# An attention and expert block on one core: a PSUM bank for the softmax denominators, three banks for the row scores, and a new order of the matmuls and copies

## The reference

```python
x = x + _layernorm(_L0_attn_ref(_layernorm(x), w_qkv, b_qkv, w_o, b_o))
x = x + _layernorm(_L0_ffn_ref(_layernorm(x), gate_w, base_w, base_b, lora_A, lora_B))
```

```python
q, k = apply_rope(q, 0), apply_rope(k, 0)
scores = jnp.einsum('bhqd,bhkd->bhqk', q, k) / math.sqrt(HEAD_DIM)
scores = jnp.where(causal, scores, -1e20)
out = jnp.einsum('bhqk,bhkd->bhqd', _softmax(scores), v)
return out @ w_o.T + b_o
```

## Time and profile before

| what | us |
|---|---|
| median of 3 runs (1070.35 to 1074.29) | 1073.55 |
| the profiled execution, its own time | 1073.55 |
| its span, first to last instruction | 1071.5 |
| what lies around the span | 2.05 |
| one group in the steady part (481.44 less 471.62, R0 to R0) | 9.82 |

### The profile page before, as it was taken

One profiled execution on the slowest core, in us unless ns is written; L12 is line 12 of the kernel. 1 busy time (PEld: TensorE's weight loads), 2 busy tenths in 40 slices (PEclk: granted clock), 3 DMA queues, 4 the chain that ended last, 5 costly groups with the idle time before them and its releaser, 6 DMA issues.

```text
span 1071.5 us, 17460 instructions
## 1 busy us (share of the span) xinstructions
PE 1026.8 (96%) x6704; PEld 843.3 (79%) x6704; DVE 614.8 (57%) x1492; ACT 397.9 (37%) x682; POOL 410.3 (38%) x461
## 2 busy tenths in 40 slices
PE   4999999999999998999999989899999999999995
PEld 3888888898886665666666658799999999999995
DVE  7354442434446675767776626566666666666654
ACT  7132221210137665776676753122222222222221
POOL 1072552433346775777776650111111122111110
PEclk8999999999999998999999999899999999999999
DMA  9144332247256776546545444122222222222201
GB/s 357 45 159 136 118 137 100 79 130 191 83 162 162 205 199 159 131 124 166 131 126 132 130 161 136 40 93 87 87 89 81 79 79 79 81 86 88 62 20 40
DMA packets 78786, 127.31 MB, mean 119 GB/s; under 512 B 7792, under 2 KB 47088, under 8 KB 75632
## 3 DMA queue, kind: packets, MB, share of 16 engines
q1 hardware_dynamic: 78704, 126.19, 39.0%
HBM read 85.27 MB, written 40.37 MB: 117 GB/s over the span
## 4 chain that ended last, share of the span: by engine, by line
PE 87%; DVE 4%; DMA 3%; POOL 2%; ACT 2%; issue 1%; SPq 1%; POOLq 0%; DVEq 0%; ACTq 0%
PE bank L1235 19%; PE bank L1237 19%; PE bank L1236 19%; PE bank L1308 7%; PE bank L1334 7%; PE bank L1348 6%; PE bank L1365 5%; PE bank L1314 2%; PE bank L1444 1%; DMA q_t<-shift_l 1%; DVE ln_st L928 1%; PE bank L1244 1%; DMA den_i<-inv_scratch 1%; POOL turn L656 1%; POOL turn L659 1%
## 5 line engine op out<-in xcount | busy, mean ns | idle before, releaser
L642 POOL TENSOR_TENSOR ln_rs<-ln_ve,minus_half 128x1 f32<-128x1 f32 x64 | 61.5, 961 | 413.7 <-DVE ln_mm L933 413.7
L989 DVE CUSTOM_DVE_ANT_0 bank<-bank,row_mask 128x384 f32<-128x384 f32 (+1 forms) x240 | 143.0, 653 | 86.2 <-PE bank L1308 86.2
L815 ACT ACTIVATE prob<-bank 128x512 f32<-128x512 f32 x320 | 172.8, 600 | 40.7 <-PE bank L1334 40.7
L1235 PE MATMUL bank<-xt_h,wq_h 128*128 128x512 f32 x320 | 128.0, 400 | 4.5 <-DVE wq_l L953 4.5
L1235 PE MATMUL bank<-wf_h,xt_h 128*128 128x384 f32 (+1 forms) x384 | 129.8, 338 | 1.8 <-DVE z L1146 1.8
L1237 PE MATMUL bank<-wf_l,xt_h 128*128 128x384 f32 (+1 forms) x384 | 130.2, 339 | 0.0
L1236 PE MATMUL bank<-wf_h,xt_l 128*128 128x384 f32 (+1 forms) x384 | 130.0, 339 | 0.0
L1308 PE MATMUL bank<-k_t,q_t 96*128 96x384 f32 (+3 forms) x512 | 127.0, 328 | 0.0
L1237 PE MATMUL bank<-xt_l,wq_h 128*128 128x512 f32 x320 | 125.8, 393 | 0.0
L1236 PE MATMUL bank<-xt_h,wq_l 128*128 128x512 f32 x320 | 125.8, 393 | 0.0
L683 POOL TENSOR_SCALAR_AFFINE_SELECT prob<-prob 128x512 f32<-128x512 f32 x128 | 83.0, 651 | 91.2 <-ACT prob L815 91.2
(11 more groups left out here) (108 smaller groups left out, 1973.0 us busy)
## 6 DMA issues: line engine op xcount, KB each, us to landing
q_t<-q_scratch SPq DMA_DIRECT2D x32, 512.0 KB, 5.3
q_scratch<-turn_h SPq DMA_DIRECT2D x16, 512.0 KB, 2.7
q_scratch<-turn SPq DMA_DIRECT2D x16, 512.0 KB, 2.9
q_t<-q_scratch SPq DMA_DIRECT2D x32, 256.0 KB, 5.5
att_scratch<-att SPq DMA_DIRECT2D x32, 256.0 KB, 2.6
at_raw<-att_scratch SPq DMA_DIRECT2D x16, 512.0 KB, 3.7
x<-x SPq DMA_DIRECT2D x16, 512.0 KB, 4.3
out<-z SPq DMA_DIRECT2D x15, 512.0 KB, 2.9
```

The lines of the kernel that those rows point to most:

```text
L642: nc.gpsimd.tensor_tensor(ln_rs[j][:], ln_ve[j][:], minus_half[:], ALU.pow).then_inc(count, 1)
L815: nc.scalar.activation(prob[n % 2][:, i, :, :].rearrange("p h q -> p (h q)"), bank[3 + (NS * n + i) % 3][:], ACT.Exp, scale=INV_SQRT_HD).t ...
L989: nc.vector.tensor_tensor_reduce(out=scored, in0=scored, in1=row_mask[:, SEQ - w:SEQ], scale=1.0, scalar=LOWEST, op0=ALU.add, op1=ALU.max, ...
L1235: mm(dst, a_h, w_h, start=start, stop=False, skip_group_check=True)
```

## The change

The denominators get bank 7 for themselves. The row scores' ring has banks 0, 1 and 2 left, so a unit waits for the one three places back. D waits for the copy of the denominators of the group before it, and V0 for the copy of the values before it, instead of the other way round. The list of TensorE is written anew, with S and R mostly taking turns, and R6 ahead of D. ACT's list changes: the shift ahead of e2, the values' copy from ahead of e3 to ahead of e5, the weight piece behind e5, the denominators' copy from ahead of e6 to ahead of e7, and `split_att(0)` ahead of e4.

```diff
--- before.py
+++ after.py
@@ -57,22 +57,18 @@
 LN = 3
 
 
-ORDER = ("S0 R0 R1 S1 S2 R2 T V0 V1 V2 V3 R3 R4 "
-         "S3 S4 S5 R5 D S6 R6 R7 S7 R8 S8 S9 R9 R10").split()
-ROW_BANKS = (0, 1, 2, 7)
-
 PRIME_AT, PRIME_STEP = 13, 3
 
 
 def ring_units():
 
-    step = [(what[0], int(what[1:] or 0)) for what in ORDER if what[0] in "RT"]
+    step = [("R", 0), ("R", 1), ("R", 2), ("T", 0)] + [("R", i) for i in range(3, NR)]
     units = [("R", 0, i, i % 2) for i in range(NR)]
     for n in range(-1, NG):
         for at, (kind, i) in enumerate(step):
             group = n + 2 if kind == "R" else n + 1
             if group < NG:
-                units.append((kind, group, i, (NR + at) % 2 if n < 0 else ROW_BANKS[at % len(ROW_BANKS)]))
+                units.append((kind, group, i, (NR + at) % 2 if n < 0 else at % 3))
     return units
 
 
@@ -834,29 +830,25 @@
             def copy_sums(n):
                 act.wait_ge(den_ps, n + 1)
                 wait(act, den_stored, 16 * n)
-                nc.scalar.copy(den_sb[:], bank[6][:]).then_inc(den_ready, 1)
+                nc.scalar.copy(den_sb[:], bank[7][:]).then_inc(den_ready, 1)
 
             for n in range(NG):
                 if n == NG - 1:
                     split_ffn(1)
                 exps(n, 0)
                 exps(n, 1)
-                exps(n, 2)
                 if n + 1 < NG:
                     shift_to_hi(n + 1)
-                if n > 0:
-                    copy_values(n - 1)
-                exps(n, 3)
-                exps(n, 4)
-                if n == NG - 2:
-                    split_att(0)
-                if 1 <= n <= NPIECE:
-                    piece_hi(n - 1)
-                exps(n, 5)
-                if n > 0:
-                    copy_sums(n - 1)
-                for i in range(6, NS):
+                for i in range(2, NS):
+                    if i == 4 and n == NG - 2:
+                        split_att(0)
+                    if i == 5 and n > 0:
+                        copy_values(n - 1)
+                    if i == 7 and n > 0:
+                        copy_sums(n - 1)
                     exps(n, i)
+                    if i == 5 and 1 <= n <= NPIECE:
+                        piece_hi(n - 1)
                 if n == NG - 5:
                     split_ffn(0)
 
@@ -1339,7 +1331,7 @@
 
                 b, g = n // KV, n % KV
                 if kc == 0:
-                    wait(pe, den_ready, n)
+                    wait(pe, att_ready, n)
                     pe.wait_ge(v_loaded[b % 2], 16 * (b // 2) + 16)
                 first, last_of = FIRST[kc], FIRST[kc] + TT - kc
                 pe.wait_ge(prob_ready, NS * n + last_of)
@@ -1355,14 +1347,14 @@
 
                 pe.wait_ge(prob_masked, TT * n + TT)
                 pe.wait_ge(prob_summed, 3 * n + 3)
-                pe.wait_ge(att_ready, n + 1)
+                wait(pe, den_ready, n)
                 p, total = prob[n % 2], key_sum[n % 2]
                 for i in range(4):
                     for h in range(REP):
                         what, at, w = ((p[:, 0:2, h, :], 0, 2), (total[:, :, h, :], 2, 2),
                                        (p[:, FIRST[1]:FIRST[1] + 1, h, :], 1, 1),
                                        (p[:, FIRST[2]:FIRST[3] + 1:2, h, :], 2, 2))[i]
-                        last = mm(bank[6][HD * h:HD * h + HD, P * at:P * (at + w)].rearrange("p (b q) -> p b q", q=P),
+                        last = mm(bank[7][HD * h:HD * h + HD, P * at:P * (at + w)].rearrange("p (b q) -> p b q", q=P),
                                   ones[:], what, start=(i == 0), stop=(i == 3), skip_group_check=True)
                 last.then_inc(den_ps, 1)
 
@@ -1415,6 +1407,9 @@
                                    wo_l[:, cols], c == 0, c == KC - 1)
                 last.then_inc(o_ps, 1)
 
+            order = ("S0 R0 S1 R1 S2 R2 T V0 V1 V2 V3 S3 R3 S4 R4 S5 R5 R6 D "
+                     "S6 R7 S7 R8 S8 R9 S9 R10").split()
+
             def step2(n, what):
 
                 kind, i = what[0], int(what[1:] or 0)
@@ -1430,7 +1425,7 @@
                     denominators(n - 1)
 
             for n in range(NG + 1):
-                for what in ORDER:
+                for what in order:
                     step2(n, what)
                 if n == NG - 2:
                     project_out(0, 0)
```

## The result

The changed kernel takes 1082.42 us (median of 5 runs, 1080.29 to 1083.33), the kernel before in the same comparison 1070.68 (1070.31 to 1074.29). The ratio is 1.0097 with a 95% interval of 1.0079 to 1.0115: about 10 us slower, 0.8 to 1.2% (the two medians are 11.7 us apart). 1087 with 1079 to 1095 was forecast. The profiled execution took 1081.9 us for a span of 1079.9, that is 8.4 us more than the profiled one of before.

What follows compares the result with a forecast made beforehand. TensorE, busy for 96% of the span, was taken to bound the kernel. Terms of 8.7 + 5.5 - 1.2 + 0.4 = +13.4 us on the profiled 1073.55 us gave 1087 us, range 1079 to 1095.

Steps and rivals of the forecast that it cites:

- S0 waits for e7, 28 times: At the next group's S0: released late by exponential e7 behind the denominators' copy, 0.31 us a group, 8.7 us.
- R6 waits for R3's maximum, 29 times: Ahead of D: with three row banks R6 waits for DVE's maximum of R3, 0.19 us a group, 5.5 us.
- own bank in the steady part: Steady groups: D and V no longer wait for each other's copies, worth nothing since neither waited before.
- the end, to the second block's first matmul: End of the loop: the last D's 5.0 us wait goes, first transpose waits 3.8; -1.2 us, bounded by +0.5 and -2.9.
- DMA burst at group 10: SyncE waits for the later denominators' copy, so group 10's shift row lands later: +0.4 us, bounded by 0 and 0.9.
- start, last group, the kernel's end: For the first and the last group nothing was taken, within 0.5 us either way.
- The ring behind S0: Three row banks after S0: R0 to R2 have 0.1 to 0.4 us in hand behind S0's new wait, no cost.
- Rival 1: Steady part stays as before and the end alone decides: 1072.3 us, or 1066.9; chance 0.08.
- rival 2: Weight loads stay covered at waiting matmuls, successor following after 0.23; waits of 0.20 and 0.08, +7.1, 1080.7 us; chance 0.15.
- Rival 3: Ring tighter than counted: T, or R1 and R2, wait as well, 0.25 us a group more, 1094 us; chance 0.11.
- Rival 4: Pauses in each group cost the clock, 1.7 us each, 49 us more, 1136 us; chance 0.02.
- but what is late next?: After the last D: the first transpose waits for ACT's y, done at 649.3, so TensorE waits 3.8 us.

Runs made afterwards that it cites:

- 8: Changed kernel with R3 ahead of S3 and R4 ahead of S4 in the list of matmuls: ratio 1.0057 to the kernel before, 1078.51 us.
- experiment 2: Kernel before with the new list of matmuls alone, four ring banks and ACT's old list kept: ratio 1.0008, 1074.53 us.
- 1: Changed kernel with ACT's denominators' copy behind e7 instead of ahead of it: ratio 1.0079 to the kernel before, 1082.27 us.
- 3: Kernel before with the banks alone (denominators in bank 7, three ring banks), old matmul order and ACT list: ratio 1.0052, 1079.83 us.
- 9: Changed kernel with R3, R4 ahead of S3, S4 and the denominators' copy behind e7: ratio 1.0028 to the kernel before, 1077.07 us.
- 4: Kernel before with the last group's values copied ahead of the first normalisation: ratio 0.9929, 1065.85 us.
- 5: Changed kernel with the last group's D again waiting for ACT's copy of its values: ratio 1.0151 to the kernel before, 1088.26 us.
- 6: Kernel before with the two bias rows (1 MB together) loaded six groups later, in group 14's turn: ratio 0.9957, 1067.46 us.

## Why the prediction was right, and what it missed

| step of the prediction | forecast us | measured us |
|---|---|---|
| S0 waits for e7, 28 times | 0.31 each, 8.7 | 0.35 each, 9.8 |
| R6 waits for R3's maximum, 29 times | 0.19 each, 5.5 | 0.20 each, 5.8, with 0.05 of each from the new order |
| own bank in the steady part | 0 | 0 (D and V wait in neither profile) |
| the end, to the second block's first matmul | -1.2 | +0.4 |
| behind it, the second tile | not foreseen | -7.1 |
| DMA burst at group 10 | +0.4 | -1.4 in this pair of profiles, not settled |
| start, last group, the kernel's end | 0 | +0.8 |
| sum | +13.4 | +8.3 |

Between the two profiles the sum is 5.1 us below the forecast: a term of -7.1 was missing, and the others together were 2 us too low. The measured time lies in the range although one path was not foreseen at all; as far as the end goes, that is luck.

**The two steady waits** are right in place and cause, and 8 put R6's to the test alone. Their sum was 8% low, 0.50 against 0.546, nearly all at S0: e7 starts 0.02 early, but S0 comes 0.08 late (2.26 against 2.18), since it starts 0.14 behind e7's end (489.10) where the prediction took 0.06. R0 behind it is 0.04 late (2.56 against 2.52). That R6's term fits so well is partly chance: the prediction put the new order's paces at nothing, and they are 0.05 of the 0.20. Against the 1.62 us of experiment 2, R6's wait itself is 0.15. (For the kernel before, e7 ends 1.78 behind S6 in the trace, not near 1.73; nothing hangs on it.)

**The ring behind S0** was weighed too lightly. The prediction gave R0 to R2 0.1 to 0.4 us in hand "behind the new wait at S0", which was right as long as that wait stood; 1 shows that without it 0.17 of the 0.35 us stays. So of the change's 0.55 us a group, the ring of three banks accounts for about 0.33 (0.15 to 0.16 at R6, 0.17 at R0), ACT's list for 0.18 on top of it (10.37 less 10.19 [experiment 1]), and the order for 0.04. At S0 the two overlap, so the split depends on which is taken out first: with the ring left at four banks, ACT's list would by the rows cost the whole wait at S0, which no run shows. 3 shows 0.48 for the ring with the old order.

**The rivals.** Rival 1 (cover is enough) and rival 2 (weight loads stay covered, 1080.7 us) fall with the round of 10.37: the latter asked for 10.1. Its own sign fails too: R0 follows the waiting S0 after 0.30 us (489.25 to 489.55) and D follows R6 after 0.38, where they take 0.23 and 0.27 in experiment 2. That the measured time lies near rival 2's is chance, by the item that it lacked as well. Rival 3 (a tighter ring) falls in the changed kernel: from R0 to V0 it is 2.09 us (489.55 to 491.64), before 2.08, so R1, R2 and T do not wait. Its wait at R0 appears only when S0's is taken out (1, 9). Rival 4 falls: of the two pauses in each of 28 or 29 groups none was followed by the lower clock; the granted clock is 1.00 from 421 to 665 us, and 19 rounds behind group 11 differ by about 0.05 us at most.

**The end** is where the prediction missed, in the step "but what is late next?". It asked this of TensorE's next wait only and stopped there. The queue that D's semaphore also releases is SyncE's: two weight loads, the last stores, the x rows, the attention rows and the reciprocals stand there in a row, and the last of these bounds the second transpose of the kernel before. The row was in the trace, as a wait of 4.2 us at line 1444 in the list that I cut to three rows; I took it for the kernel's end. For the same reason the prediction says that the clock fell behind the waits of 4.0 and 5.0 us alone: it fell behind this one too (1.97 us at 675.66 for a transpose that takes 1.04 at full clock). 4 and 5 show the worth of the wait: 7.6 us (0.0071 x 1073) in the old kernel, 5.8 in the new.

In the part that was foreseen, y came 1.7 us later than I had it against the statistics, so that TensorE waited 5.5 us and not 3.8, since POOL's two small operations took 1.60 and 0.84 us there instead of 0.55 and 0.19. DVE's weight split starts at once in the changed kernel (662.05), as ACT's casts are no longer held up by the denominators' copy. The Trainium skill (SBUF — State Buffer, Who interferes with whom) says that a VectorE operation with two inputs in SBUF contends with GpSimd's reads; the trace agrees: line 638 takes 0.55 us with DVE idle (677.43) and 1.60 beside the split.

**Group 10** stays partly open. That the wait there is the burst is shown by 6. That it was shorter in the changed kernel's profile (2.19 against 3.99 us) is not explained by the change: experiment 4, with the same loop as before, has 2.3, and 5, with the same loop as the changed kernel, 2.9; the others have 1.7 (3), 3.0 (2 and 8), 4.8 (1) and 5.3 (9). So it differs between executions of what is in this stretch the same program, and may be part of the spread between the runs of one kernel (1068.7 to 1078.2 us for the kernel before over all comparisons), which I did not test.

## What to carry to other kernels

Taking a buffer from a ring that shows no waits is not free: write down, unit by unit, when the consumer is done and when the producer comes back, for the whole round, and do it again with each wait taken out, since the first late one hides the next. When a semaphore comes earlier or later, follow every queue that waits for it, the DMA queue above all, to the next tile and not only to the next wait of the bound engine. A wait that occurs once, at a seam, can be worth as much (5 us, 7.6 with what hangs on it) as one that repeats in every group (5.8 and 9.8 us here), and a copy moved ahead of a normalisation and a weight cast was all it took.

## What the runs showed of the hardware that was not expected

- A wait of 0.1 to 0.4 us at a matmul does not appear as idle time of TensorE in the list of waits, but as one in that of the weight loads, partly as "issue". For the score matmuls "issue" went from 3.7 us to 31.9 while the line of ACT's exponentials fell from 13.4 to 2.9, so the lines are to be read together, and against the starts in the timeline.
- POOL's operation on 128 x 1 elements is stretched from 0.55 to 1.60 us and from 0.19 to 0.84 beside a two-input DVE operation (rows of the changed kernel at 662.21 and 663.89).
- The DMA wait at group 10 varied between 1.7 and 5.3 us in profiles of kernels that issue the same transfers in the same order, and was gone with 1 MB moved out of the burst (6).
